# Rebuilding the setup of a two-layer transformer kernel and moving its weight splits and its weight fold into the first batch's slots

## The reference

```python
x = L0_attn_query                                   # (8, 256, 256) float32
xn = layernorm(x)
x = x + attn0(xn) + ffn0(xn)
xn = layernorm(x)
x = x + attn1(xn) + ffn1(xn)

# attn0: 16 heads of 128, causal; q, k, v = xn @ w + b; softmax(q k^T / sqrt(128)) v @ w_o + b_o
# ffn0: float8 (e4m3) operands, bf16 results, 1024 hidden:
#       (gelu(xn8 @ wg8[0]) * (xn8 @ wg8[1])) as float8 @ wl8
# attn1: 16 heads of 16, no mask, with biases
# ffn1: h = fwht(xn * SU_ug) / 64; up = h @ W_up.T * (Ws_ug[:1024] * 64); gate likewise
#       y = fwht(silu(gate) * up * SU_dp) / 64 @ W_down.T * (Ws_dp * 64)
```

## Time and profile before

| | |
|---|---|
| three runs | 956.63, 958.75, 959.01 us (median 958.75) |
| profiled execution | 958.63 us, span in the trace 956.8 us |
| mean granted clock of TensorE | 0.937 of 2.4 GHz |
| busy in the span | PE 830.6 (87%), PEld 609.9 (64%), DVE 742.3 (78%), ACT 689.1 (72%), POOL 471.4 (49%) |
| chain that ended last | PE 68%, DVE 9%, ACT 3%, issue 2%, DMA 1% |
| DMA | 100.97 MB, mean 106 GB/s |

### The profile page before, as it was taken

How to read it: one execution, slowest core, us unless ns; L and a number is a source line. 1 busy time by engine, 2 the same in 40 slices (tenths; PEclk the granted TensorE clock), 3 DMA queues, 4 the chain that set the end, 5 groups by cost and what they waited for, 6 DMA issues and landing times.

```text
span 956.8 us, 21194 instructions
## 1 busy us (share of the span) xinstructions
PE 830.6 (87%) x7120; PEld 609.9 (64%) x7120; DVE 742.3 (78%) x2028; ACT 689.1 (72%) x1973; POOL 471.4 (49%) x734
## 2 busy tenths in 40 slices
PE   3555538999899999999999999999999999996763
PEld 1123225687677777777777777777777777764541
DVE  6988855766768788887878787878787878875684
ACT  2654625656669778887888888788778878884673
POOL 1443332412326565665666555656565656566452
PEclk9675778999999999999999999999999999998896
DMA  9543412212243456554564555455556554544454
GB/s 331 196 148 110 133 52 82 52 34 43 48 103 75 90 93 140 102 83 108 123 105 78 115 116 111 77 124 102 107 80 143 89 101 89 123 98 93 114 107 102
DMA packets 283179, 100.97 MB, mean 106 GB/s; under 512 B 241344, under 2 KB 281024, under 8 KB 281920
## 3 DMA queue, kind: packets, MB, share of 16 engines
q1 hardware_dynamic: 280368, 97.27, 45.9%
q10 hardware_dynamic: 2704, 2.36, 0.7%
HBM read 30.38 MB, written 10.49 MB: 43 GB/s over the span
## 4 chain that ended last, share of the span: by engine, by line
PE 68%; DVE 9%; ACT 3%; issue 2%; DMA 1%; POOL 1%; SPq 0%; POOLq 0%; DVEq 0%; ACTq 0%
PE ps L666 42%; PE ps L716 9%; PE ps L816 4%; PE ps L799 4%; PE ps L692 3%; DVE arena L660 2%; PE ps L825 2%; PE ps L801 2%; PE ps L729 2%; DVE arena L999 1%; ACT arena L655 1%; DMA arena<-arena 1%; ACT arena L875 1%; DVE arena L659 1%; DVE nb L1006 1%
## 5 line engine op out<-in xcount | busy, mean ns | idle before, releaser
L660 DVE SCALAR_TENSOR_TENSOR arena<-ps,bqk,arena 128x256 bf16<-128x256 f32 x416 | 187.4, 479 | 63.3 <-ACT arena L655 61.8
L666 PE MATMUL ps<-arena,wqkv 128*128 128x256 bf16 x1728 | 215.2, 275 | 6.5 <-PEq L210 6.5
L655 ACT ACTIVATE arena<-ps,bqk 128x256 bf16<-128x256 f32 x416 | 177.9, 466 | 30.0 <-PE ps L666 20.8
L666 PEld LDWEIGHTS ps<-arena,wqkv 128*128 128x128 bf16 x1728 | 161.7, 98 | 48.1 <-issue 28.3
L1174 POOL TENSOR_SCALAR arena<-arena,rc 128x128 f32<-128x128 f32 (+1 forms) x256 | 106.3, 428 | 174.4 <-DVE rc L1022 174.4
L875 ACT ACTIVATE arena<-arena,nb 128x128 f32<-128x128 f32 (+1 forms) x256 | 114.3, 447 | 90.0 <-DVE nb L999 89.4
L1165 POOL TENSOR_TENSOR arena<-arena 128x512 bf16<-128x512 f32 x107 | 124.8, 1167 | 69.8 <-ACT arena L654 69.8
L1181 POOL TENSOR_SCALAR arena<-arena,rc 128x256 f32<-128x256 f32 x256 | 120.1, 483 | 75.7 <-DVE rc L1026 75.7
L654 ACT ACTIVATE arena<-arena 128x384 bf16<-128x384 f32 (+1 forms) x256 | 136.6, 572 | 18.7 <-POOL arena L1181 9.8
L875 ACT ACTIVATE arena<-ps,nb 128x256 f32<-128x256 f32 x256 | 118.6, 473 | 13.3 <-DVE nb L1006 10.8
L716 PE MATMUL ps<-wo,arena 128*128 128x256 bf16 x768 | 105.6, 274 | 10.5 <-DVE arena L660 9.8
(11 more groups left out here) (98 smaller groups left out, 1286.4 us busy)
## 6 DMA issues: line engine op xcount, KB each, us to landing
arena<-scratch_qk SPq DMA_DIRECT2D x96, 64.0 KB, 2.2
arena<-arena SPq DMA_TRANSPOSE x256, 2.7
scratch_qk<-arena SPq DMA_DIRECT2D x32, 128.0 KB, 1.9
arena<-in_x SPq DMA_DIRECT2D x4, 512.0 KB, 8.6
arena<-in_w_gating SPq DMA_DIRECT2D x2, 1024.0 KB, 6.7
arena<-in_w_q SPq DMA_DIRECT2D x2, 1024.0 KB, 8.6
scratch_xT<-arena ACTq DMA_DIRECT2D x8, 256.0 KB, 6.4
arena<-in_w_k SPq DMA_DIRECT2D x2, 1024.0 KB, 6.4
```

Of the source, the lines that this page charges most:

```text
L655: return nc.scalar.activation(out, in_, ACT.Identity, bias=bias)
L660: return nc.vector.scalar_tensor_tensor(out=out, in0=in_, scalar=bias, in1=hi, op0=ALU.add, op1=ALU.subtract)
L666: last = nc.tensor.matmul(out, lhsT, rhs, start=(n == 0), stop=(n == len(steps) - 1))
```

## The change

It touches nearly all of the setup. No operation of the mathematics changes except the way in which the biases `bo0` and `bo1` are added.

- **Buffers.** Layer 0's buffers and `cur` lie at the start of `arena`; everything of the setup lies behind them, over layer 1's buffers. So the first batch's layer 0 may run while the setup ends. There is one block and no barrier. `x` has three buffers of a pair each, the normalised rows one.
- **FFN loop.** gelu is one tile late, the product is GpSimd's and the float8 cast two tiles late; the `w_linear` product is in one piece after tile 3 of the next pair, the transposes after tile 5. The last pair's `w_linear` product and its output copy stand in slot 0.
- **Chunks.** They are cut anew (`qk` holds four heads' q and k columns with both k halves). `g8` needs only its first half for tiles 0 to 3. Two of the thirteen splits stay in the setup (tiles 18 and 24), eleven go to the end of slots 0 to 13, and eight loads to slots 1 to 11, ahead of the slot's transposes on SP's queue.
- **Fold** goes from slots 1 to 15 (and 16 to 19) into 13 to 24 (and 25, 26).
- **Biases.** GpSimd splits `bo0`, `bo1` into three bf16 parts, VectorE copies them into rows 0, 32 and 64 of `brow`, and the matmul that opens an output bank is ones by `brow`. `rows_after` and the buffer `x1` go; `x1_sum` writes in place.
- The first pair's halves are written straight into `cur`, with no store and load.

```diff
-        WORDS = 26240
+        WORDS = 25728
+        FIRST1 = 4 * T + 8 * HD0 * TT + 3 * S3 + 4 * S3 + 2 * T + 2 * KD * T
...
-        carve = carver(0)
+        carve = carver(FIRST1)
+        stage = carve(3 * 2048, F32, "p (a n) -> p a n", a=3)
...
+        chunks = [("g8", 0), ("g8", 1), ("l8", 0), ("qk", 0), ("v", 0), ("wo0", 0), ("qk", 1), ("qk", 2), ("v", 1),
+                  ("qk", 3), ("wo0", 1), ("l1", 0), ("wo1", 0), ("ug", 0), ("ug", 1), ("dn", 0)]
+        split_slot = {("wo0", 0): 0, ("qk", 1): 1, ("qk", 2): 3, ("v", 1): 4, ("qk", 3): 6, ("wo0", 1): 7, ("l1", 0): 9,
+                      ("wo1", 0): 10, ("ug", 0): 11, ("ug", 1): 12, ("dn", 0): 13}
+        split_tile = {("qk", 0): 18, ("v", 0): 24}
+        pool_low = (("qk", 1), ("qk", 2), ("qk", 3), ("wo1", 0), ("ug", 1))
+        load_slot = {("v", 1): 1, ("qk", 3): 2, ("wo0", 1): 4, ("l1", 0): 5, ("wo1", 0): 7, ("ug", 0): 8, ("ug", 1): 10,
+                     ("dn", 0): 11}
...
+        def pool_setup(pool):
...
+            def product(n):
+                pool.wait_ge(gelu_done, n + 1)
+                pool.wait_ge(lin_done, n + 1)
+                upto(pool, a8_done, n - 1)
+                nc.gpsimd.tensor_tensor(ab[:, n % 2, :], ge[:, n % 2, :], f1[:, n % 2, :], ALU.mult
+                                        ).then_inc(prod_done, 1)
...
+            for n in range(NT):
+                p, k = divmod(n, KH)
+                product(n)
+                if k == 3 and p + 1 < PAIRS:
+                    rstd_of(p + 1)
+                if k == 5 and p:
+                    join(p - 1)
+            join(PAIRS - 1)
+
+        def act_setup(act):
...
+            input_high(0)
+            for n in range(NT):
+                p, k = divmod(n, KH)
+                gate(n)
+                if n:
+                    gelu(n - 1)
+                if k == 6 and p + 1 < PAIRS:
+                    input_high(p + 1)
+                if k == 4 and p:
+                    output(p - 1)
+                for c in splits:
+                    if split_tile.get(c) == n:
+                        split_high(act, c)
+            gelu(NT - 1)
...
+        def dve_setup(dve):
...
+            def activation8(n):
+                p, k = divmod(n, KH)
+                dve.wait_ge(prod_done, n + 1)
+                upto(dve, d0_ps, p - 1)
+                nc.vector.tensor_copy(a8[:, p % 2, k, :], ab[:, n % 2, :], saturate=False).then_inc(a8_done, 1)
...
+            statistics(0)
+            float8(("g8", 0))
+            normalise(0)
+            input_low(0)
+            float8(("g8", 1))
+            for n in range(NT):
+                p, k = divmod(n, KH)
+                linear_gate(n)
+                if n >= 2:
+                    activation8(n - 2)
+                if n == 1:
+                    float8(("l8", 0))
+                if k == 2 and p + 1 < PAIRS:
+                    statistics(p + 1)
+                if k == 4 and p + 1 < PAIRS:
+                    normalise(p + 1)
+                if k == 6 and p + 1 < PAIRS:
+                    input_low(p + 1)
+                for c in splits:
+                    if split_tile.get(c) == n:
+                        split_low_dve(dve, c)
+            activation8(NT - 2)
+            activation8(NT - 1)
+            dve.wait_ge(bo_left, 2)
+            for r, part in ((0, bo_hi), (32, bo_mid), (64, bo_rest)):
+                for i in range(2):
+                    last = nc.vector.tensor_copy(brow[r:r + 1, :, i * D:(i + 1) * D], part[r:r + 1])
+            last.then_inc(bias_rows, 1)
...
+        def pe_setup(pe):
...
+                if p and m == 3:
+                    for i in range(4):
+                        pe_linear0(pe, p - 1, i)
+                if m == 5 and p + 1 < PAIRS:
+                    transposes(p + 1)
...
-        FOLD_UP = (1, 3, 5, 7)
-        FOLD_DOWN = range(8, 8 + KH)
+        FOLD_UP = (13, 14, 15, 16)
+        FOLD_DOWN = range(17, 17 + KH)
...
-                nc.tensor.matmul(ps[:, bank, :], zeros[:, 0:P], zeros[:, :], start=True, stop=False)
+            def open_bank(bank, closing=False):
+                nc.tensor.matmul(ps[:, bank, :], ones[:, :], brow[:, int(bank != BK_X or closing), :], start=True,
+                                 stop=False)
...
+                if n == 0:
+                    pe.wait_ge(gate_done, NT)
...
             for s in range(SLOTS):
+                for c in loads_in[s]:
+                    load_chunk(sp, c)
...
+                for c in splits_in[s]:
+                    split_high(act, c)
+                if s == 0:
+                    act_last_output(act)
```

More of the change, by code:

```diff
@@ L145, in build @@
         rows_stored = sem("rows_stored")
-        STG = 3
-        PAIRS = B // 2
-        NG = PAIRS * KH
-        chunks = [("g8", 0), ("g8", 1), ("l8", 0)]
-        chunks += [(w, k) for w in (0, 1, 2) for k in range(KD)]
-        chunks += [("wo0", 0), ("wo0", 1), ("l1", 0), ("wo1", 0), ("ug", 0), ("ug", 1), ("dn", 0)]
-        slot_of = {c: n % STG for n, c in enumerate(chunks)}
-        turn_of = {c: n // STG + 1 for n, c in enumerate(chunks)}
-        splits = [c for c in chunks if c[0] not in ("g8", "l8")]
@@ L1159, in dve_program @@
                     result(b)
+                for c in splits_in[s]:
+                    if c not in pool_low:
+                        split_low_dve(dve, c)
+                if s == 2:
+                    dve_constants(dve)
                 fold(s)
@@ L1302, in _ @@
             def _(sp):
+                sp_setup(sp)
                 sp_program(sp)
```

753 lines of the change are left out of this document (373 added, 380 removed).

## The result

| | before | after |
|---|---|---|
| median of six runs each | 957.65 us (956.63 to 959.01) | 965.15 us (963.22 to 967.76) |
| profiled execution, span | 958.63, 956.8 us | 963.39, 961.6 us |
| slot 0 begins | 144.58 | 108.89 |
| first maximum | 151.07 | 120.92 |
| seventeenth (16 slots) | 232.46 (81.4) | 226.74 (105.8) |

The ratio is 1.0076, 95% interval 1.0058 to 1.0094: slower, where 950 us and "faster" were forecast. The times of the maxima come from the timeline, as in the earlier trace rows; of sixteen slots means from the first maximum to the seventeenth. Against the forecast's 949.7 for the profiled execution, 963.39 is 13.7 us more: slot 0 comes 7.9 late (forecast 101), slot 0 itself takes 12.0 and not 11, the sixteen slots 105.8 and not 103.9, the down steps 8.5 and not 8.7, the rest of the steady stage 0.5 less than before, and the last stretch 2.6 us more than before instead of 1.1 less.

A forecast was written before the change was run, and what follows sets the result against it. VectorE was taken to bound the setup's feed-forward tiles, TensorE the steady stage. From 958.63 us, 7.8 left after setup gain and first-batch costs and 1.1 of tail were subtracted: 949.7, say 950; range 936 to 968.

The forecast's parts named there:

- Tile 1.75 us: Setup's feed-forward loop: GpSimd product 1.16 plus VectorE cast 0.43 make at least 1.6 us per tile, 1.75 with semaphores.
- the lock: VectorE's work between two SBUF buffers and GpSimd's work exclude each other, whichever started first; work reading PSUM is free.
- The crossing: Setup, from tile 5's products to the next pair's first: 6.5 us at full clock, 8.5 at half.
- The product on GpSimd: Setup loop: GpSimd's bf16 product of 512 columns, taken as 1.16 us, could be 0.8 or 1.6.
- The sixteen slots: First batch, first to seventeenth maximum: 103.9 us, against 81.4 before.
- The splits' terms: Weight splits in the first batch's slots: 8.8 us with low half on VectorE, 12.7 us with it on GpSimd.
- The transfers' term: First batch: eight loads ahead of the DMA transposes on SP's queue cost 1.8 us, between 0 and 16.
- The up steps' term: Fold's four up steps, now in neighbouring first-batch slots: 8.1 us, against 4.3 before.
- The clock's 4 us: First batch: TensorE busy 3 to 4.3 us of 6 us slots, so its clock may fall for parts: 4 us.
- The forecast's sign for slots 1 to 12: Profile sign of being right: mean clock of slots 1 to 12 above 0.85.
- The rival of the fallen clock: Slots 1 to 15: clock falls, ten plain slots at half cost 10 us, folds some 12; 968 us, chance 0.2.
- The tail: Behind the last maximum: GpSimd's last bias addition goes, so VectorE's cast is not stretched: 1.1 us gained.

The follow-up runs named there:

- a_early2: `a_copy` with the next pair's statistics, power and normalisation issued earlier in pairs 0 and 1, and one store moved ahead of a load: 957.61 us, 5.5 less.
- a_prod_dve: `a_copy` with the setup's product made by VectorE instead of GpSimd: 955.69 us, 7.4 less.
- a_no_splits: `a_copy` with the slots' eleven weight splits cut to the last 8 columns of each row: sixteen slots 84.4 us, 22.2 less than 106.6.
- a_loads: `a_copy` with each first-batch slot's weight load issued behind its turns, not ahead of them: 958.38 us, 4.7 less.
- with copies: Kernels whose DMA transposes of the probabilities are plain copies of 256-byte pieces, transposition left out: kernel before 956.79 us, changed kernel 963.09 us.
- the fastest one: `a_copy` with earlier normalisation, product on VectorE, loads behind turns, two fold buffers, and 288 unused bytes in front of the arena: 937.93 us.
- a_copy: The changed kernel with plain copies of 256-byte pieces in place of its DMA transposes: 963.09 us.
- a_fold2: `a_copy` with a second buffer (gl) for the fold's up steps: 959.72 us, 3.4 less.
- b_copy_b: The kernel before with plain copies of 256-byte pieces in place of its DMA transposes: 956.79 us.

## Why the prediction was wrong

**The loop.** "Tile 1.75 us" holds where tiles flow (gate copies 1.2 to 1.9 us apart), and the lock showed as forecast: the casts' median is 0.42 us, but their mean is 0.72 and the longest takes 1.74. VectorE's load fell as said.

**The crossing** is the step that failed. The prediction wrote 1.0 + 0.9 + 1.2 + 1.0 + 2.4 = 6.5 us, 8.5 at half clock, and took the normalisation for done when the transposes come: it has no term for a wait there. It isn't: statistics, power, normalisation and transposes are a chain over three engines, each link queued behind a tile's work, and it ends 3.7 us after tile 5 is done (53.35 to 57.03). With it 11.3 to 12.1 us were paid three times, 9.4 us in all over the forecast. `a_early2` removes that wait in two of the three crossings and gets 7.6 us of slot 0 back. The first pair was 5.3 us longer than its term and started 1.1 late, the second 1.8, the third 2.6, the last 3.0 shorter: +7.8, which is the 7.9 of the table. What the prediction weighed was how long an instruction lasts; what it left out was the queue position of the one that releases it.

**The product on GpSimd** was priced right (1.15 for 1.16 us). What the sum left out is that the product also stands in the crossing: it holds the power back in GpSimd's queue, and beside it the normalisation lasts 2.20 us, where the first pair's (at 9.13 us, with no product beside it) takes 1.38. VectorE, whose load it was to relieve, would have needed 0.42 us, and `a_prod_dve` is 7.4 us faster.

**Slot 0** 12.0 for 11: right within 1 us.

**The sixteen slots** 105.8 for 103.9. The splits' terms, 8.8 and 12.7, make 21.5; `a_no_splits` shows 22.2, but some 4 of them lie in slot 3, which `a_loads` frees too, and a part is the clock's; so the splits by themselves may cost nearer 18, and the close match is partly luck. The transfers' term of 1.8 was too small: putting the loads behind the turns gave 4.7 us. The up steps' term of 8.1 was too small too: without splits, slots 13 to 16 take 28.3 us, 11.2 over four plain slots of 4.28. The clock's 4 us can't be set apart: it did fall, to 0.90 in the mean of the sixteen slots, and one slot cost 1.6 us more at 0.65 than at 0.86. The forecast's sign for slots 1 to 12, a mean above 0.85, came true with 0.88. The rival of the fallen clock (968) comes close in time and is not what happened: it wanted ten plain slots at half clock, and in the profile no slot's mean is under 0.68. In slots 9 to 12 the clock stayed at 1.00 although TensorE waited 8.9 us there. So 105.8 for 103.9 is near by terms whose errors cancel in part.

**Down steps behind** 8.5 for 8.7: right.

**The tail** was forecast 1.1 us shorter and was 2.6 longer. The saving itself may well be there: with copies and the unshifted start the changed kernel's tail is 99.7 us and its base's 100.5, 0.8 less, in one profile each. What the prediction had no term for is the start of the arena, though the replacement of the buffers ahead of it stands in the diff. Moving it alone costs the kernel before 4.1 us with copies, 3.5 of them in the tail; in the changed kernel the same comparison gives 2.6 us, of which 0.9 in the tail, not clear of noise, and in the fastest one 2.8, with 4.0 in the tail of its profile. With real transposes the start was not moved alone, so how much of the tail's 3.7 us is its doing stays open.

**As a whole**: forecast and measurement are 15 us apart, and the runs with single edits give back 5.5 (place of the normalisation), 4.7 (order of loads and turns), 3.4 (buffer of the fold) and 2.6 (start of the arena). These are gains over the kernel after and not all of them errors of the sum; the largest error is the crossing's 9.4. The change gained 35.7 us at the start of slot 0 and spent 24.4 in the sixteen slots, 8.5 in the next sixteen, 5.5 in slot 0 itself and 2.5 in the tail. The range (936 to 968) held the result; the sign was wrong.

## What to carry to other kernels

When a step is moved, follow its releaser's place in each queue and not only its length: a wait of TensorE for a short operation can be a whole chain over three engines. Order a queue by who waits: small transfers on which TensorE stands go ahead of large ones that are needed slots later. And when buffers ahead of a large one are changed, look at the address at which it then starts.

## What was not expected of the hardware

- **The start of a buffer.** Moved by 224 bytes, the same 105 GB/s take 0.48 of the DMA engines' time and not 0.40, a read of 64 KB lands in 2.8 us and not 2.3, and the kernel before with copies takes 4.1 us more.
- **The clock of the first batch isn't the same in every execution.** The same slot with the same work ran at a mean of 0.86 in `a_copy` and 0.65 in `a_fold2`, whose programs are equal up to slot 13. Single executions of `a_copy` spread over 8.4 us, those of `b_copy_b`, in whose profile the clock is 1.00 in each of the sixteen slots, over 3.1. That the clock makes this spread is likely but not shown: one execution of each kernel was profiled.
- **Gains in separate stretches of one chain add**: 13.6 us by single edits, 13.5 together, within an uncertainty of some 4 us.
